# Routed attention: values taken in ten turns of a unit's 36 blocks, one turn across two rows' ends, and a weights' ring 15 slots deep

## The chip, the cores and the metric

One core of one Trainium2 chip. The metric is the device time of the program in microseconds. The kernel before has a median of 668.74 us over 3 runs (668.3 to 669.78).

## What is computed

`x` is 2 x 1024 tokens of 512 numbers. After a layer norm two attentions run on it and both are added to `x`:

- a local one, 16 query heads of 32 on 4 key heads, with biases, RMS norm, rotary position and a window of 64 keys back, then an output projection;
- a routed one. Each token has 16 heads of keys and values, of which a gate picks one (`argmax`), so all 16 query heads share one key and one value per token:

```
k_shared = einsum('bth,bthd->btd', indicator, k)
v_shared = einsum('bth,bthd->btd', gating_top1, v)
att = einsum('bhqd,bkd->bhqk', q, k_shared) / sqrt(hd)
att = softmax(where(causal, att, -inf))
y = einsum('bhqk,bkd->bhqd', att, v_shared)
```

The change is in the routed attention alone. All is float32, some matmuls in the float32r form.

## The kernel before, in words

The program has two stages. The first (layer norm, projections, local attention, output projection) ends where the routed attention begins, at 388.67 us of the profiled span. The order of the work on every engine comes from a planner (`make_plan`, then `Routed.run`), which keeps a model of the engines' times and writes out one list of steps; each engine's program walks this list and emits its own part of each step, with semaphore waits. TensorE executes in that order.

**Units, rows and blocks.** The routed attention is cut into 8 units u (4 groups of 4 heads by 2 batches). A unit has 8 rows i of 128 queries; row i has i + 1 key blocks j, the diagonal first, so 36 blocks k in all (`PRODUCTS`). The steps:

- `row_scores` (TensorE L1055, out `s_ps`, 4 banks): scores of a later unit, only for their row maxima, which VectorE takes (L1321, L1324). 48 for each unit but the first.
- `key_scores` (TensorE L1088, out `st_ps`, 3 banks): one float32r matmul of 512 columns for each block. ScalarE takes the exponential (L1545) into the weights' ring `p_t[k % RING]`, 12 slots; GpSimd zeroes what lies above the diagonal (L1684) and adds the weights of two neighbouring blocks into one of 6 `p_sum` buffers (L1697; in the last unit VectorE, L1350).
- `key_values` (TensorE L1104, out `od_ps`): for each block 4 matmuls of 32 output partitions, one for each head; the trace has 8 records for a block (a float32 matmul shows as two), and `key_sums` (L1118) the same for the row sums, one for each pair of blocks.
- `row_done` (ScalarE L1558): copy of a row's values and sums out of `od_ps`, 128 x 256.
- `finish` (TensorE L1127, out `s_ps`): two transposes, then VectorE divides (L1366, L1368); after every fourth row the residual is added and the unit's result is stored at its end.

**Turns.** TensorE takes `key_values` in turns of several blocks, between which it issues row scores, key scores and finishes. `value_group` cuts them inside a row: the row's rest when that is at most 5 blocks, else 4. That gives 1, 2, 3, 4, 5, 4 + 2, 4 + 3, 4 + 4: eleven turns a unit, 88 in all. A turn that begins a row waits for the copy of the row before (`ro_r`), since every row uses the same half, `od_ps[:, 0:2, :]`.

`Routed.run` takes the way that can start first of four: finish, maximum, key scores, values, with ties going in that order. Key scores are ready when a `st_ps` bank is free, the ring slot of 12 blocks before has been read and one of the 6 pair buffers is free; a turn of values when all its blocks are scored, its weights are ready and, for a row's start, the last copy is done.

Of the kernel before, what the change touches and what calls it, by code (L numbers as in the profile page):

```python
# [7 lines left out]
P = 128  # L8
D = 512
KC = D // P  # L10
H, HKV, DK = 16, 4, 32
# [68 lines left out]
HOP = 0.2  # L80

SLACK = 0.6
VALUES_AT_ONCE = 4

Q_LANDS = 6.0

# [379 lines left out]
    return p  # L466


def value_group(k):

    left = row_end(PRODUCTS[k][0]) - k + 1
    return left if left <= VALUES_AT_ONCE + 1 else VALUES_AT_ONCE


class Routed:
# [106 lines left out]
    def next_values(self):  # L582
        n = len(PRODUCTS)
        if self.valued == UNITS_ROUTED * n:
            return None
        u, k = divmod(self.valued, n)
        end = self.valued + value_group(k)
        if end > self.scored:
            return None
        whats = [self.done["weights", m] for m in range(self.valued, end)]  # L590
        i, j = PRODUCTS[k]
        if i == j:
            whats.append(self.values_free)
        if ends_row(k + value_group(k) - 1):
            whats += [self.done["pair", end - m] for m in (1, 2) if ("pair", end - m) in self.done]
        return max(whats)

    def take_values(self):
        n = len(PRODUCTS)
        self.now += TURN  # L600
        u, k = divmod(self.valued, n)
        _, hg, b = self.unit(u)
        i, j = PRODUCTS[k]
        for g in range(k, k + value_group(k)):
# [3 lines left out]
        if ends_row(g):  # L608
            for m in row_sums(i):
                self.do("key_sums", u, b, m)  # L610
                self.now += 0.22
                if m in PAIR_OF:
                    self.done["pair used", u * len(PAIR_OF) + PAIR_OF[m]] = self.now + HOP
                else:
                    self.done["sum", u * n + m] = self.now + HOP
            self.do("row_done", u, b, i)
# [3 lines left out]
        self.valued += g + 1 - k  # L620
        self.now += TURN

    def next_finish(self):
# [89 lines left out]
def mixed_attention_kernel(nc, counts, x, w_tok, w_qt, w_o, b_qkv, b_o, w_norm, scale, rope, ident, mask, rows, rank,  # L713
# [188 lines left out]
    def tensor_program(e):  # L902
        lane = Lane(e)
        for step, *key in plan.steps:
# [168 lines left out]
            elif step == "key_scores":  # L1073
                u, b, k = key
                i, j = PRODUCTS[k]
                if k == 0:
                    lane.wait_ge(*M["r_row"].of(u))
                    lane.wait_ge(*M["r_row_lo"].of(u))
                if u == 0:
                    lane.wait_ge(*queries(u, i))  # L1080
                if k >= ST_BANKS:
                    lane.wait_ge(*M["rp_exp"].of((u, k - ST_BANKS)))
                elif u:
                    lane.wait_ge(*M["rp_exp"].of((u - 1, len(PRODUCTS) - ST_BANKS + k)))
                else:

                    lane.wait_ge(*M["p_t_r"].of((*last_tile, k + 1)))
                e.matmul(st_ps[k % ST_BANKS][:, :, :], k_stack[0:HALVES + 2, b * S + j * P:b * S + (j + 1) * P],  # L1088
                         q_op[b][0:HALVES + 2, i, :, :], start=True, stop=True).then_inc(
                             *M["rst_mm"].did((u, k)))  # L1090

            elif step == "key_values":
                u, b, k = key
                i, j = PRODUCTS[k]
                if i == j:
                    lane.wait_ge(*M["rp_diag"].of((u, i)))
                    if i or u:
                        lane.wait_ge(*M["ro_r"].of((u, i - 1) if i else (u - 1, IT - 1)))
                    else:
                        lane.wait_ge(*M["at_lo"].of(last_tile))  # L1100
                else:
                    lane.wait_ge(*M["rp_exp"].of((u, k)))
                for h in range(HQ):
                    mm = e.matmul(od_ps[h * DK:(h + 1) * DK, 0, :], v_all[:, b * IT + j, 0:DK],  # L1104
                                  p_t[k % RING][:, h, :], start=i == j, stop=ends_row(k))
                mm.then_inc(*M["rpv"].did((u, k)))

            elif step == "key_sums":
                u, b, k = key
                i, j = PRODUCTS[k]  # L1110
                if k in PAIR_OF:
                    lane.wait_ge(*paired(u, k))
                    weights = p_sum[(u * len(PAIR_OF) + PAIR_OF[k]) % SUMS]
                else:
                    weights = p_t[k % RING]
                first = k == row_sums(i)[0]
                for h in range(HQ):
                    mm = e.matmul(od_ps[h * DK:(h + 1) * DK, 1, :], v_all[:, b * IT + j, DK:VW], weights[:, h, :],  # L1118
                                  start=first, stop=ends_row(k))
# [12 lines left out]
    def vector_program(e):  # L1132
# [3 lines left out]
        for step, *key in plan.steps:  # L1136
# [201 lines left out]
            elif step == "key_scores":  # L1338
                u, b, k = key
                i, j = PRODUCTS[k]  # L1340
                p = p_t[k % RING]
                if k in PAIR_OF and SUMMER[u] == "V":
                    lane.wait_ge(*M["rp_exp"].of((u, k)))
                    if PRODUCTS[k - 1][1] == i:
                        lane.wait_ge(*M["rp_diag"].of((u, i)))
                    n = u * len(PAIR_OF) + PAIR_OF[k]
                    if n >= SUMS:
                        w, was = divmod(n - SUMS, len(PAIR_OF))
                        lane.wait_ge(*M["rsum"].of((w, ENDS_PAIR[was])))
                    e.tensor_tensor(p_sum[n % SUMS][:, :, :], p_t[(k - 1) % RING][:, :, :], p[:, :, :],  # L1350
                                    ALU.add).then_inc(*M["rp_pair_v"].did((u, k)))

            elif step == "finish":
# [26 lines left out]
    def scalar_program(e):  # L1380
# [12 lines left out]
        for step, *key in plan.steps:  # L1393
# [135 lines left out]
            elif step == "key_scores":  # L1529
                u, b, k = key  # L1530
                lane.wait_ge(*M["rst_mm"].of((u, k)))
                if u == 0 and k < RING:

                    if k < 2 * RING_P_LOC:
                        lane.wait_ge(*M["p_t_r"].of((*last_tile, QUADS - 1)))
                    elif k < 2 * RING_P_LOC + QUADS:
                        lane.wait_ge(*M["pv_mm"].of(last_tile))
                    else:
                        lane.wait_ge(*M["gemm_read"].of((ROUNDS - 1, *LAST_UNIT)))
                if k >= RING or u:  # L1540
                    w, was = (u, k - RING) if k >= RING else (u - 1, len(PRODUCTS) - RING + k)
# [3 lines left out]
                e.activation(p_t[k % RING][:, :, :], st_ps[k % ST_BANKS][:, :, :], ACT.Exp, scale=ROUTED_SCALE).then_inc(  # L1545
                    *M["rp_exp"].did((u, k)))
# [21 lines left out]
    def gpsimd_program(e):  # L1568
# [6 lines left out]
        for step, *key in plan.steps:  # L1575
# [101 lines left out]
            elif step == "key_scores":  # L1677
                u, b, k = key
                i, j = PRODUCTS[k]
                p = p_t[k % RING]  # L1680
                if i == j:
                    lane.wait_ge(*M["rp_exp"].of((u, k)))
                    e.nop(nofuse=True)
# [3 lines left out]
                elif k in PAIR_OF and SUMMER[u] == "G":  # L1687
# [9 lines left out]
                    e.tensor_tensor(p_sum[n % SUMS][:, :, :], p_t[(k - 1) % RING][:, :, :], p[:, :, :],  # L1697
                                    ALU.add).then_inc(*M["rp_pair"].did((u, k)))

            elif step == "finish":  # L1700
# [223 lines left out]
```

## Time and profile before

| what | value |
|---|---|
| median of 3 runs | 668.74 us (668.3 to 669.78) |
| the profiled execution's own time | 671.4 us |
| its span | 669.5 us |
| mean granted TensorE clock | 0.993 |
| routed attention on TensorE | 388.67 to 664.02 us |
| TensorE, weight loads, VectorE, ScalarE, GpSimd busy | 95, 76, 68, 54, 66% of the span |

In the rows below PE is TensorE's matmuls and PEld its weight loads, DVE VectorE, ACT ScalarE, POOL GpSimd. Matmul ends are modelled, so the argument goes by starts. A group such as `x3` runs from its first start to its last modelled end.

### The profile page before, as it was taken

The numbers are of one execution on the slowest core, as the hardware profiler recorded it, in microseconds if no ns is written. First come the engines' busy times: TensorE is split into PE (matmuls) and PEld (weight loads), VectorE is DVE, ScalarE is ACT, GpSimd is POOL, SyncE is SP. The second block draws the span as 40 slices with busy tenths as digits, with TensorE's granted clock in tenths as the row PEclk, the third lists the DMA queues.
The fourth block names the chain that finished last, engine by engine and source line by source line (L and its number), as shares of the span: only waits on it lengthen the run. The fifth ranks groups of instructions, "written<-read, shape, count | busy, mean of one in ns | idle before, by whom it ended". The sixth has DMA issues, their size and how long they took to land.

```text
span 669.5 us, 19210 instructions
## 1 busy us (share of the span) xinstructions
PE 637.4 (95%) x7432; PEld 509.8 (76%) x7432; DVE 455.8 (68%) x1184; ACT 361.7 (54%) x906; POOL 442.4 (66%) x384
## 2 busy tenths in 40 slices
PE   4699999999999999999999899999999999999997
PEld 3587788887888888888778677777777777777675
DVE  3966457657665675656664388887878787878454
ACT  5357355625544445535257455656565565656684
POOL 3876856368654749382895467776878687868730
PEclk9999999999999999999999899999999999999999
DMA  9524222241223133212216631503214131302011
GB/s 315 197 60 112 60 77 79 76 122 41 78 70 91 50 94 104 78 39 75 64 33 166 163 96 58 137 26 93 71 51 113 51 111 36 104 29 89 4 34 33
DMA packets 64939, 56.59 MB, mean 85 GB/s; under 512 B 6480, under 2 KB 48848, under 8 KB 64848
## 3 DMA queue, kind: packets, MB, share of 16 engines
q1 hardware_dynamic: 62704, 54.45, 27.9%
q8 instruction: 58, 0.95, 0.6%
q10 hardware_dynamic: 2144, 0.93, 0.5%
q14 instruction: 33, 0.27, 0.1%
HBM read 37.20 MB, written 17.89 MB: 82 GB/s over the span
## 4 chain that ended last, share of the span: by engine, by line
PE 88%; DVE 5%; ACT 2%; DMA 2%; issue 2%; SPq 0%; ACTq 0%; DVEq 0%
PE gemm L946 20%; PE s_ps L1055 12%; PE od_ps L1104 11%; PE st_ps L1088 10%; PE gemm L1032 7%; PE gemm L942 6%; PE od_ps L1118 5%; PE win L1006 4%; PE win L991 3%; PE s_ps L1127 2%; PE av L1018 2%; DMA raw<-w_tok 2%; PE av L1045 1%; PE tp L957 1%; PE tp L913 1%
## 5 line engine op out<-in xcount | busy, mean ns | idle before, releaser
L946 PE MATMUL gemm<-w_tok,xt 128*128 128x512 f32 (+1 forms) x768 | 184.0, 380 | 5.4 <-DVE g_exp L1188 2.2
L946 PEld LDWEIGHTS gemm<-w_tok,xt 128*128 128x128 f32 x768 | 129.6, 191 | 28.5 <-DVE g_exp L1188 2.7
L1055 PE MATMUL s_ps<-k_stack,w_tok 96*128 96x512 f32 (+2 forms) x336 | 100.0, 381 | 0.3 <-DVE x_res L1286 0.3
L1088 PE MATMUL st_ps<-w_tok,k_stack 98*128 98x512 f32 x288 | 98.9, 413 | 0.2 <-ACT p_loc L1545 0.2
L1545 ACT ACTIVATE p_loc<-st_ps 128x512 f32<-128x512 f32 x144 | 77.6, 599 | 35.9 <-PE st_ps L1088 34.7
L1321 DVE TENSOR_REDUCE picked_fk<-s_ps 128x1 f32<-128x512 f32 x112 | 72.3, 684 | 9.0 <-PE s_ps L1055 8.9
L1497 ACT ACTIVATE p_loc<-win,l_max 128x96 f32<-128x96 f32 x256 | 60.9, 390 | 31.1 <-DVE l_max L1260 31.1
L1055 PEld LDWEIGHTS s_ps<-k_stack,w_tok 96*128 96x128 f32 x336 | 54.9, 188 | 24.6 <-issue 8.8
L1642 POOL TENSOR_TENSOR rope_b<-qkv,sin_t 128x128 f32<-128x128 f32 (+1 forms) x32 | 27.5, 880 | 65.5 <-DVE qkv L1238 65.5
L1666 POOL TENSOR_TENSOR p_loc<-p_loc,l_rec 128x1536 f32<-128x1536 f32 x16 | 44.1, 2758 | 36.4 <-DVE l_rec L1272 36.4
L1324 DVE CUSTOM_DVE_ANT_0 s_ps<-s_ps,x_ln,picked_fk 128x128 f32<-128x128 f32 (+3 forms) x112 | 56.8, 555 | 9.7 <-PE s_ps L1055 9.7
L1324 DVE CUSTOM_DVE_ANT_0 s_ps<-s_ps,x_ln 128x128 f32<-128x128 f32 (+3 forms) x112 | 51.8, 521 | 16.2 <-PE s_ps L1055 15.9
L1545 ACT ACTIVATE p_loc_t<-st_ps 128x512 f32<-128x512 f32 x96 | 52.3, 599 | 18.9 <-PE st_ps L1088 18.6
L942 PE MATMUL gemm<-xt,w_qt 128*128 128x256 f32 x384 | 55.0, 291 | 4.5 <-DVE g_exp L1188 2.8
L1088 PEld LDWEIGHTS st_ps<-w_tok,k_stack 98*128 98x128 f32 x288 | 50.6, 189 | 9.8 <-ACT p_loc L1545 2.1
L1618 POOL TENSOR_TENSOR rms_y<-rms_v,minus_half 128x20 f32<-128x20 f32 x16 | 56.5, 3534 | 1.3
L1032 PE MATMUL gemm<-w_o,attn_t 128*128 128x512 f32 x192 | 54.0, 414 | 2.4 <-DVE attn_t L1277 2.4
L942 PEld LDWEIGHTS gemm<-xt,w_qt 128*128 128x128 f32 x384 | 50.1, 195 | 7.6 <-DVE g_exp L1188 3.3
L1104 PE MATMUL od_ps<-p_loc,v_all 128*32 128x128 f32 x1152 | 44.3, 277 | 0.0
L1506 ACT ACTIVATE p_loc_t<-win 96x512 f32<-96x512 f32 x64 | 36.7, 638 | 13.8 <-PE win L1006 12.8
L1684 POOL TENSOR_SCALAR_AFFINE_SELECT p_loc<-p_loc 128x512 f32<-128x512 f32 x40 | 25.0, 634 | 25.3 <-ACT p_loc L1545 25.3
L1032 PEld LDWEIGHTS gemm<-w_o,attn_t 128*128 128x128 f32 x192 | 34.3, 193 | 9.4 <-issue 3.1
(172 smaller groups left out, 1295.4 us busy)
## 6 DMA issues: line engine op xcount, KB each, us to landing
w_tok<-q_parts SPq DMA_DIRECT2D x72, 128.0 KB, 2.6
q_parts<-qt SPq DMA_DIRECT2D x120, 64.0 KB
x_ln<-x SPq DMA_DIRECT2D x8, 512.0 KB, 4.6
x_res<-x SPq DMA_DIRECT2D x16, 256.0 KB, 2.8
partial<-x_res SPq DMA_DIRECT2D x16, 256.0 KB, 2.3
w_tok<-partial SPq DMA_DIRECT2D x8, 512.0 KB, 5.2
raw<-w_tok SPq DMA_DIRECT2D x3, 1024.0 KB, 12.5
v_win<-v_rows SPq DMA_DIRECT2D x64, 48.0 KB, 2.2
```

Of the source, the lines that this page charges most:

```text
L942: i = e.matmul(g[:, 0:PAIR], w_qt_p[r][:, k, a * P:(a + 1) * P], xs[l][:, k, :], start=first, stop=last)
L946: i = e.matmul(g[:, 0:cols], xs[l][:, k, a * P:(a + 1) * P], w_tok_p[r][:, k, c0:c0 + cols], start=first, stop=last)
L1032: i = e.matmul(gemm[bank][:, :], attn_t[l][:, kc, :], w_o_p[r][:, kc, :], start=kc == 0 and q == 0, stop=kc == KC - 1 and q == 2)
L1055: e.matmul(s_ps[bank][:, 0:cols], q_op[b][0:HALVES, i, h, :], k_stack[0:HALVES, b * S + c0:b * S + c0 + cols], start=True, stop=True).then ...
L1088: e.matmul(st_ps[k % ST_BANKS][:, :, :], k_stack[0:HALVES + 2, b * S + j * P:b * S + (j + 1) * P], q_op[b][0:HALVES + 2, i, :, :], start=T ...
L1104: mm = e.matmul(od_ps[h * DK:(h + 1) * DK, 0, :], v_all[:, b * IT + j, 0:DK], p_t[k % RING][:, h, :], start=i == j, stop=ends_row(k))
L1321: e.tensor_reduce(dst, s[:, 0:cols], AX.X, ALU.max).then_inc(*M["rs_max"].did((u, t)))
L1324: e.tensor_tensor_reduce(out=s[:, 0:cols], in0=s[:, 0:cols], in1=causal[:, S - width + c0:S - width + c0 + cols], scale=1.0, scalar=dst if ...
L1497: i = e.activation(p_loc[a][:, g, quad, :], win[:, g, quad * KEYS:(quad + 1) * KEYS], ACT.Exp, bias=l_max[:, a, n:n + 1])
L1545: e.activation(p_t[k % RING][:, :, :], st_ps[k % ST_BANKS][:, :, :], ACT.Exp, scale=ROUTED_SCALE).then_inc(*M["rp_exp"].did((u, k)))
L1618: e.tensor_tensor(rms_y[:, :], rms_v[:, :], minus_half[:, :].to_broadcast([P, NH]), ALU.pow).then_inc(*M["rms_r"].did((n, a)))
L1666: e.tensor_tensor(p_l, p_l, l_rec[:, a, :].unsqueeze(2).to_broadcast([P, H, KEYS]), ALU.mult).then_inc(*M["p_r"].did((m, a)))
```

## The change

It replaces the rule of the turns by a table of ten sizes, of which the first covers rows 0 and 1 (1 + 2 blocks); the other nine are the sizes of before. In a turn all values come first, then all sums, then the copies of the rows that end in it. Rows alternate between the two halves of the bank `od_ps`; a row's copy waits for the sums of the last row of its turn, and a turn's first diagonal waits for the copy of the row before the turn. The ring has 15 slots, three more in rooms that the first stage has left (two in `k_t`, one in `picked_fv`), and its slot goes on counting from unit to unit, since 36 is no multiple of 15.

```diff
-RING = 12
+RING = 15
+
+TURN_SIZES = (3, 3, 4, 5, 4, 2, 4, 3, 4, 4)
+TURN_OF = {}
+for _n in TURN_SIZES:
+    TURN_OF.update(dict.fromkeys(range(len(TURN_OF), len(TURN_OF) + _n), (len(TURN_OF), len(TURN_OF) + _n - 1)))
...
-def value_group(k):
-
-    left = row_end(PRODUCTS[k][0]) - k + 1
-    return left if left <= VALUES_AT_ONCE + 1 else VALUES_AT_ONCE
+def turn_end(k):
+
+    return TURN_OF[k][1] + 1
+
+
+def rows_ended(k):
+
+    return [i for i in range(IT) if k <= row_end(i) < turn_end(k)]
...
+def ring(u, k):
+    return (u * len(PRODUCTS) + k) % RING
...
-        whats = [self.done["weights", m] for m in range(self.valued, end)]
-        i, j = PRODUCTS[k]
-        if i == j:
-            whats.append(self.values_free)
-        if ends_row(k + value_group(k) - 1):
-            whats += [self.done["pair", end - m] for m in (1, 2) if ("pair", end - m) in self.done]
+        whats = [self.done["weights", m] for m in range(self.valued, end)] + [self.values_free]
+        whats += [self.done["pair", u * n + m] for i in rows_ended(k) for m in row_sums(i) if m in PAIR_OF]
...
+    keys_room = Room(k_t)
+    p_t += [keys_room.piece(HQ, P) for _ in range(2)] + [Room(picked["fv"]).piece(HQ, P)]
...
-                    if i or u:
-                        lane.wait_ge(*M["ro_r"].of((u, i - 1) if i else (u - 1, IT - 1)))
+                    first = PRODUCTS[TURN_OF[k][0]][0]
+                    if first or u:
+                        lane.wait_ge(*M["ro_r"].of((u, first - 1) if first else (u - 1, IT - 1)))
...
-                    mm = e.matmul(od_ps[h * DK:(h + 1) * DK, 0, :], v_all[:, b * IT + j, 0:DK],
-                                  p_t[k % RING][:, h, :], start=i == j, stop=ends_row(k))
+                    mm = e.matmul(od_ps[h * DK:(h + 1) * DK, 2 * (i % 2), :], v_all[:, b * IT + j, 0:DK],
+                                  p_t[ring(u, k)][:, h, :], start=i == j, stop=ends_row(k))
...
-                lane.wait_ge(*M["rsum"].of((u, row_end(i))))
+                lane.wait_ge(*M["rsum"].of((u, row_end(max(rows_ended(turn_of_row(i)[0]))))))
...
-                e.activation(o_sb[i % 2][:, :, :], od_ps[:, 0:2, :], ACT.Copy).then_inc(*M["ro_r"].did((u, i)))
+                e.activation(o_sb[i % 2][:, :, :], od_ps[:, 2 * (i % 2):2 * (i % 2) + 2, :], ACT.Copy).then_inc(*M["ro_r"].did((u, i)))
```

## Rows read from the trace of the kernel before

**Rows 1.** The page: span and busy time.

```profile
span 669.5 us, 19210 instructions
...
PE 637.4 (95%) x7432; PEld 509.8 (76%) x7432; DVE 455.8 (68%) x1184; ACT 361.7 (54%) x906; POOL 442.4 (66%) x384
```

**Rows 2.** The page: the chain that ended last, shares by engine.

```profile
PE 88%; DVE 5%; ACT 2%; DMA 2%; issue 2%; SPq 0%; ACTq 0%; DVEq 0%
```

**Rows 3.** Windows: stretch, PE, PEld, DVE, ACT, POOL busy (x), clock, DMA share, GB/s.

```profile
388.67:664.02 275.35, 274.38 (x4326) 204.44 (x4325) 212.31 (x702) 173.05 (x352) 195.18 (x185) 1.00 0.24 65
425.44:609.66 184.22, 183.66 (x2766) 137.21 (x2765) 149.87 (x510) 113.33 (x231) 142.47 (x135) 1.00 0.28 75
626.87:662.22 35.35, 35.04 (x675) 25.70 (x674) 15.25 (x37) 27.65 (x58) 15.00 (x17) 1.00 0.07 18
```

**Rows 4.** Waits in the routed stage: who waited for whom, total us, times, longest.

```profile
PEld od_ps L1104 <- issue: 22.0, 78, 0.4
```

**Rows 5.** Timeline of PE: one turn of values in the last unit.

```profile
652.85 0.97 PE L1088 MATMUL st_ps<-w_tok,k_stack 98*128 98x512 f32 x3
653.74 0.64 PE L1104 MATMUL od_ps<-p_loc_t,v_all 128*32 128x128 f32 x16
...
654.42 0.40 PE L1118 MATMUL od_ps<-bias_o,v_all 128*32 128x128 f32 x8
654.64 0.40 PE L1118 MATMUL od_ps<-cos_t,v_all 128*32 128x128 f32 x8
654.97 0.96 PE L1088 MATMUL st_ps<-w_tok,k_stack 98*128 98x512 f32 x3
```

**Rows 6.** Timeline of PE: a gap with row scores and seven key scores.

```profile
600.38 1.19 PE L1055 MATMUL s_ps<-k_stack,w_tok 96*128 96x512 f32 x4
601.41 0.62 PE L1088 MATMUL st_ps<-w_tok,k_stack 98*128 98x512 f32 x2
601.93 0.47 PE L1055 MATMUL s_ps<-k_stack,w_tok 96*128 96x512 f32 x1
602.24 0.39 PE L1088 MATMUL st_ps<-w_tok,k_stack 98*128 98x512 f32 x1
...
604.41 0.30 PE L1055 MATMUL s_ps<-k_stack,w_tok 96*128 96x256 f32 x1
604.64 0.62 PE L1104 MATMUL od_ps<-p_loc_t,v_all 128*32 128x128 f32 x13
```

**Rows 7.** Timeline of PE: a gap without row scores and with five key scores.

```profile
635.21 0.96 PE L1088 MATMUL st_ps<-w_tok,k_stack 98*128 98x512 f32 x3
636.40 0.98 PE L1088 MATMUL st_ps<-w_tok,k_stack 98*128 98x512 f32 x2 [0.22 <-ACT p_loc L1545]
637.31 0.43 PE L1104 MATMUL od_ps<-p_loc_t,v_all 128*32 128x128 f32 x8
```

**Rows 8.** Windows of L1088 alone: stretch, PE busy (x key scores), PEld busy (x).

```profile
626.87:662.22 35.35, 14.94 (x45) 7.35 (x45) 1.00 0.07 18
611.27:613.82 2.55, 0.80 (x2) 0.38 (x2) 1.00 0.47 144
425.44:609.66 184.22, 62.96 (x186) 32.90 (x185) 1.00 0.28 75
...
600.30:604.64 4.34, 2.43 (x7) 1.32 (x7) 1.00 0.31 93
```

**Rows 9.** Timeline, all engines: end of row 1's turn, its copy, row 2's turn.

```profile
642.48 0.40 PE L1118 MATMUL od_ps<-bias,v_all 128*32 128x128 f32 x8
642.81 0.96 PE L1088 MATMUL st_ps<-w_tok,k_stack 98*128 98x512 f32 x3
642.94 0.39 ACT L1558 ACTIVATE rope_b<-od_ps 128x256 f32<-128x256 f32 x1
643.92 0.54 PE L1104 MATMUL od_ps<-p_loc,v_all 128*32 128x128 f32 x12
```

**Rows 10.** Windows of L1055 alone, the same columns: row scores in the long gap.

```profile
600.30:604.64 4.34, 3.29 (x9) 1.60 (x9) 1.00 0.31 93
```

More of the change, by code:

```diff
@@ L82 @@
 SLACK = 0.6
-VALUES_AT_ONCE = 4
 Q_LANDS = 6.0
@@ L586, in next_values @@
         u, k = divmod(self.valued, n)
-        end = self.valued + value_group(k)
+        end = u * n + turn_end(k)
         if end > self.scored:
             return None
-        whats = [self.done["weights", m] for m in range(self.valued, end)]
-        i, j = PRODUCTS[k]
-        if i == j:
-            whats.append(self.values_free)
-        if ends_row(k + value_group(k) - 1):
-            whats += [self.done["pair", end - m] for m in (1, 2) if ("pair", end - m) in self.done]
+        whats = [self.done["weights", m] for m in range(self.valued, end)] + [self.values_free]
+        whats += [self.done["pair", u * n + m] for i in rows_ended(k) for m in row_sums(i) if m in PAIR_OF]
         return max(whats)
@@ L602, in take_values @@
         _, hg, b = self.unit(u)
-        i, j = PRODUCTS[k]
-        for g in range(k, k + value_group(k)):
+        rows = rows_ended(k)
+        for g in range(k, turn_end(k)):
             self.do("key_values", u, b, g)
@@ L607, in take_values @@
             self.done["values", u * n + g] = self.now + HOP
-        if ends_row(g):
+        for i in rows:
             for m in row_sums(i):
@@ L615, in take_values @@
                     self.done["sum", u * n + m] = self.now + HOP
+        for i in rows:
             self.do("row_done", u, b, i)
@@ L619, in take_values @@
             self.values_free = self.copied[u * IT + i] = self.busy(self.now + 0.1, ("A", 0.38)) + HOP
-        self.valued += g + 1 - k
+        self.valued += turn_end(k) - k
         self.now += TURN
@@ L1114, in tensor_program @@
                 else:
-                    weights = p_t[k % RING]
+                    weights = p_t[ring(u, k)]
                 first = k == row_sums(i)[0]
                 for h in range(HQ):
-                    mm = e.matmul(od_ps[h * DK:(h + 1) * DK, 1, :], v_all[:, b * IT + j, DK:VW], weights[:, h, :],
+                    mm = e.matmul(od_ps[h * DK:(h + 1) * DK, 2 * (i % 2) + 1, :], v_all[:, b * IT + j, DK:VW], weights[:, h, :],
                                   start=first, stop=ends_row(k))
@@ L1340, in vector_program @@
                 i, j = PRODUCTS[k]
-                p = p_t[k % RING]
+                p = p_t[ring(u, k)]
                 if k in PAIR_OF and SUMMER[u] == "V":
@@ L1349, in vector_program @@
                         lane.wait_ge(*M["rsum"].of((w, ENDS_PAIR[was])))
-                    e.tensor_tensor(p_sum[n % SUMS][:, :, :], p_t[(k - 1) % RING][:, :, :], p[:, :, :],
+                    e.tensor_tensor(p_sum[n % SUMS][:, :, :], p_t[ring(u, k - 1)][:, :, :], p[:, :, :],
                                     ALU.add).then_inc(*M["rp_pair_v"].did((u, k)))
@@ L1537, in scalar_program @@
                         lane.wait_ge(*M["pv_mm"].of(last_tile))
-                    else:
-                        lane.wait_ge(*M["gemm_read"].of((ROUNDS - 1, *LAST_UNIT)))
-                if k >= RING or u:
-                    w, was = (u, k - RING) if k >= RING else (u - 1, len(PRODUCTS) - RING + k)
+                    elif k < 2 * RING_P_LOC + QUADS + 2:
+                        lane.wait_ge(*M["gemm_read"].of((ROUNDS - 1, *LAST_UNIT)))
+                    elif k < 2 * RING_P_LOC + QUADS + 4:
+                        lane.wait_ge(*M["s_mm"].of(last_tile))
+                    else:
+                        lane.wait_ge(*M["picked_fv"].of(last_tile))
+                if u or k >= RING:
+                    w, was = divmod(u * len(PRODUCTS) + k - RING, len(PRODUCTS))
                     lane.wait_ge(*M["rpv"].of((w, was)))
@@ L1544, in scalar_program @@
                     lane.wait_ge(*(paired(w, done) if done in PAIR_OF else M["rsum"].of((w, done))))
-                e.activation(p_t[k % RING][:, :, :], st_ps[k % ST_BANKS][:, :, :], ACT.Exp, scale=ROUTED_SCALE).then_inc(
+                e.activation(p_t[ring(u, k)][:, :, :], st_ps[k % ST_BANKS][:, :, :], ACT.Exp, scale=ROUTED_SCALE).then_inc(
                     *M["rp_exp"].did((u, k)))
@@ L1679, in gpsimd_program @@
                 i, j = PRODUCTS[k]
-                p = p_t[k % RING]
+                p = p_t[ring(u, k)]
                 if i == j:
@@ L1696, in gpsimd_program @@
                         lane.wait_ge(*M["res_bias"].of(last_tile))
-                    e.tensor_tensor(p_sum[n % SUMS][:, :, :], p_t[(k - 1) % RING][:, :, :], p[:, :, :],
+                    e.tensor_tensor(p_sum[n % SUMS][:, :, :], p_t[ring(u, k - 1)][:, :, :], p[:, :, :],
                                     ALU.add).then_inc(*M["rp_pair"].did((u, k)))
```

2 lines of the change are left out of this document (added).

## The prediction

> **What bounds the kernel now.** I read the page's busy line and chain first: TensorE is busy 95% of the span and holds 88% of the chain that ended last [rows 1, 2]. Busy time alone proves little, so I cut the span into stretches. From 388.67 to 664.02 us, the routed stage, matmuls cover 274.38 of 275.35 us at granted clock 1.00, the upper of the two levels (2.4 GHz), while VectorE has 212.31 and ScalarE 173.05 [rows 3]. Nothing else is near full, in units 1 to 5 or in the stretch without row scores. So the stage is as long as TensorE's issue order takes, and the question is how much of it goes into switching and waiting instead of into columns. The waits give a first hint: 78 of the 88 turns begin with weight loads idle on "issue", 22.0 us together, 0.28 us each [rows 4]. It is overlapped in part, so I don't take it as the price; I take starts in the timeline.
>
> **Price of a turn.** In the chosen turn the third key score starts at about 652.85 + 0.97 - 0.39 = 653.43 (0.39 is the modelled length of a single one), the values at 653.74: 0.31 us later [rows 5, 6]. Two key scores in a row start 0.62 - 0.39 = 0.23 apart [rows 6]. Entry costs 0.08. At the end, groups of eight sums start 0.22 apart, so the next would be at 654.86; the key score comes at 654.97, 0.11 late. And three key scores behind a turn take 0.96 instead of 0.39 + 2 x 0.23 = 0.85: 0.11 more [rows 5]. Together **0.30 us a turn**. The change has 80 turns for 88: gross **-2.4 us**. The blocks' own matmuls don't change in number or shape.
>
> **What the merged turn moves.** It needs both rows' three blocks at once, two diagonal cuts and one pair sum; blocks run several ahead of values nearly everywhere, so I price this at nothing; without that lead it would cost the exponential and the cut of block 2. On ScalarE the copy of row 0 now stands directly before that of row 1, with the exponentials behind both. Row 2's turn waits for both, where it waited for one. A copy is 0.39 us. Before, it starts at 642.94, 0.46 after the last sums' first start, and row 2's turn starts at 643.92 [rows 9]. A second copy would end at 643.72, 0.20 before the turn: just covered by three key scores and a finish. I take 0; if uncovered, 8 x 0.39 = 3.1 us, the other end. The two finishes come together and take two of the four `s_ps` banks, a delay for row scores, not more of them. No DMA issue is added. Those tied to key scores (query loads on SyncE's queue) can only come earlier with a longer lead, those tied to a row's copy in unit 0 about one gap later; the first is not needed for a unit, the second for a residual added four rows later. GpSimd's cuts and sums keep number and order among themselves.
>
> The copies are also the place where a rule speaks. The Trainium skill, page "PSUM — Partial Sum Buffer", section "PSUM bank collisions raise a hardware error", says that TensorE writing and ScalarE reading one bank in the same partitions collide even at different columns. The alternation of halves inside one bank would by this buy no overlap of values and copy, and with no cover behind it the sum would be 3.1 us worse; the trace has no such overlap to judge it by.
>
> **What fewer gaps cost.** This is the counter-term. Between turns TensorE fills with row scores and key scores, and there are three `st_ps` banks. The stretch without row scores has 45 key scores in its 15 gaps, exactly three a gap [rows 8]. A unit needs 36: eleven gaps hold 33 at three each, ten hold 30, so six instead of three must be a fourth or later in a gap (or done in advance). Their price, from below and above:
> - without row scores: from the third key score at 635.21 + 0.96 - 0.39 = 635.78 to the turn at 637.31 is 1.53 us; two more at 0.23 and the way into the turn, 0.31, would be 0.77 [rows 7]. So 0.76 is lost, 0.38 for each beyond three;
> - with row scores between: the gap from 600.38 has 9 row scores and 7 key scores, 16 instructions [rows 8, 10]. 15 pitches of 0.23, 0.10 behind the turn and 0.21 from the narrow last one make 3.76; it took 4.26 [rows 6]. 0.50 over 4 is 0.12 each. The lower end is 0, since units 1 to 5 hold 186 key scores in 55 gaps, 3.4 a gap, with TensorE covering 183.66 of 184.22 us [rows 3, 8]. I take 0.05, near the lower end, because most gaps there hold a fourth key score and only the longest ones show much.
> Three more a unit, in some seven units with row scores: 21 x 0.05 = **+1.05 us** (0 to 2.5).
>
> **What the deeper ring gives.** At the start of unit 6 the gap has only two key scores [rows 8] though three banks exist: twelve slots are full. Three more slots let the lead grow there. The six pair buffers bound it next: with rows 6 and 7 holding seven pairs, about 14 blocks ahead. The lead is spent at the end, where the last 45 must fit 14 gaps (42). Before, the lead ran short once, at the 0.76 us gap [rows 7]. I take half of that back, **-0.4 us** (0 to -0.76). In unit 0 the first lap is also freer, by blocks 12 to 14; nothing before unit 0's sums depends on it, so 0.
>
> **Sum:** -2.4 + 1.05 - 0.4 = -1.75 us. The profiled execution took 671.4 us, of which 669.5 is span; it would be 669.65. The median shown is 668.74, 2.7 us below that execution, an offset I keep: **667.0 us**. Before 388.67 and behind the last turn nothing changes.
>
> **Rivals.**
> 1. *All of the saving and the long gaps too*: the lead stays high enough that later key scores cost nothing. For it: the capped gap at unit 6 shows room for more; against it: ten gaps of three are 30, not 36. -2.4 - 0.76, about 665.6.
> 2. *Turns saved, waits gained*: each unit pays 3 x 0.12 = 0.36 for 0.30 saved. Against it: VectorE and ScalarE have a fifth or more idle [rows 3]. For it: four and three banks are a shallow queue, and rows 6 show it empty. 21 x 0.12 = 2.5 against 2.4 and perhaps 0.2 from the ring: 668.6. This is also where it ends if the planner, whose order I haven't got, trades the turn for longer gaps.
> 3. *The end stretch starves (slower)*: place, the key scores from the last row score on. If the lead there isn't larger than before, 3 more key scores in this stretch and 3 in unit 6 behind it pay 0.38: 2.3 us, besides 2.5 of rival 2. +4.8 - 2.4 = 671.1. It decides where the gaps there must hold more than three; with a lead of eleven or more it doesn't come.
> 4. *Two copies in a row hold up row 2's turn*: uncovered, +3.1 on -1.75, 670.1. Against it: the 0.20 us of cover just worked out, more in units with row scores. By the bank rule above the wait can't be avoided, only covered.
> The change not doing what it says has one form, that a turn across a row's end costs a switch inside; values and sums alternate in today's turns with starts as even as within either (the 0.22 of rows 5), so I leave it out.
>
> **How the numbers follow.** Forecast 0.50, rival 1 0.13, rival 2 0.22, rival 3 0.11, rival 4 0.04. The forecast's own range is 665.9 to 667.8, from the bounds 0 and 0.12 of the later key scores narrowed by the ring's. Two tenths of a per cent, 1.3 us, is about what a measurement of this kernel can tell from no change; that is 667.4 or 670.1. Faster: 0.42 of the forecast's half and rival 1, 0.55. Slower: rival 3 and half of rival 4, 0.13. Within: 0.32. The range leaves out the far part of rival 3 and of rival 4 and a little below rival 1: 665.2 to 669.3.
>
> **What would show it.** Right: 80 groups of values instead of 88, each with 0.30 around it; unit starts about 0.15 to 0.3 us closer together; capped gaps of two gone; last turn near 660.5 instead of 662.22. A chain still on TensorE. Wrong: key scores with idle time ended by ScalarE in many gaps (rivals 2 and 3), counts of five and more in gaps without row scores (3), the weight load before row 2's first values idle on the copy (4), or unit lengths unchanged though turns are gone. If the total moves by more than 3.2 us, something other than turns moved.

## The result, and the profile after

After: **675.07 us** (673.79 to 678.17, 4 runs); before, 668.52 (668.29 to 669.78, 4 runs). The ratio is 1.0085, 95% interval 1.0048 to 1.0121: slower, by some 6 us, where 667.0 was forecast and 669.3 was the upper end of the range. The profiled execution took 674.89 us. Its page, span, busy time and chain:

```profile
span 673.6 us, 19202 instructions
...
PE 641.5 (95%) x7432; PEld 510.6 (76%) x7432; DVE 456.8 (68%) x1184; ACT 361.9 (54%) x906; POOL 445.7 (66%) x384
...
PE 86%; DVE 5%; ACT 3%; issue 2%; DMA 2%; POOL 1%; SPq 0%; ACTq 0%; DVEq 0%; POOLq 0%
```

Against [rows 1, 2] this tells little: TensorE is still busy 95% of the span, 4.1 us longer, and holds 86% of the chain for 88. So the stage has to be cut. Windows of the kernel after, by the first values of a unit: unit 0; units 1 to 5; units 6 and 7 up to the start of the last sums, in two lines; the whole stage; and a stretch behind unit 0's end. The columns are those of [rows 3]:

```profile
386.04:428.38 42.34, 40.95 (x565) 30.74 (x564) 35.36 (x123) 24.53 (x50) 28.89 (x28) 0.96 0.34 91
428.38:610.79 182.41, 181.58 (x2746) 134.02 (x2746) 142.77 (x486) 110.73 (x226) 136.33 (x129) 1.00 0.27 70
610.79:645.57 34.78, 34.67 (x574) 25.39 (x573) 21.91 (x66) 21.53 (x46) 26.21 (x26) 1.00 0.08 23
645.57:668.12 22.55, 22.28 (x445) 16.19 (x444) 14.35 (x30) 16.39 (x33) 3.08 (x5) 1.00 0.09 26
386.04:668.12 282.08, 279.48 (x4326) 206.33 (x4325) 214.39 (x702) 173.18 (x352) 194.51 (x185) 0.99 0.24 64
...
421.37:427.00 5.63, 5.63 (x19) 4.74 (x20) 4.58 (x15) 4.26 (x8) 5.35 (x6) 0.70 0.59 159
```

The kernel before: unit 0, and units 6 and 7 in two lines, of which only the sum is compared (units 1 to 5 are the second line of [rows 3]):

```profile
388.67:425.44 36.77, 36.67 (x554) 27.29 (x554) 31.54 (x112) 21.41 (x44) 23.97 (x23) 1.00 0.22 64
609.66:640.32 30.66, 30.35 (x519) 22.01 (x518) 17.64 (x51) 20.18 (x43) 23.97 (x23) 1.00 0.13 38
640.32:664.02 23.70, 23.70 (x491) 17.95 (x490) 13.27 (x31) 18.14 (x38) 4.78 (x6) 1.00 0.09 25
```

Unit 0 took 42.34 us for 36.77, units 1 to 5 182.41 for 184.22, units 6 and 7 57.33 for 54.36. The stage is +6.73: +5.6, -1.8, +3.0. (The profiled span is only 4.1 longer because the stage started 2.63 us earlier; see the last section.)

These three numbers can't be read as they stand, since the stretches don't hold the same work. A unit's first values now stand behind more scores, of its own and of the unit after it. The counts of TensorE's records in the rows say by how much: 565 for 554 in unit 0, 2746 for 2766 in units 1 to 5, 574 + 445 for 519 + 491 in units 6 and 7, so +11, -20 and +9. By starts, these are 6 key scores and 5 row scores more in unit 0, 5 and 15 fewer in units 1 to 5, 1 fewer and 10 more behind them. At 0.23 us each (an estimate, the pitch of two key scores) that moves +2.5, -4.6 and +2.1 us. At equal work unit 0 lost some 3.0 us, the five middle units 2.8, and the last two 0.9: all three stretches lost, the middle ones too.

TensorE's covered time grew too, from 274.38 to 279.48, with the same 4326 matmul records: only 2.6 us of the stage are idle, and the instructions stand further apart.

Turns themselves, waits of the weight loads, and two new waits of TensorE; then the waits of the row scores' weight loads on VectorE, after and before:

```profile
PEld od_ps L1122 <- issue: 17.7, 60, 0.5
...
PE st_ps L1105 <- DMA w_tok<-w_tok: 1.1, 1, 1.1
PE od_ps L1122 <- ACT rope_sq L1580: 0.8, 5, 0.2
...
PEld s_ps L1072 <- DVE picked_fk L1342: 11.7, 47, 0.3
...
PEld s_ps L1055 <- DVE picked_fk L1324: 5.5, 24, 0.3
```

60 turns for 78 of [rows 4] begin with that idle time, 0.30 us each. The second line is where the matter shows: a key score waits for the DMA that brings the row of maxima of its unit. That wait is in no group of the prediction. The third is a turn that waits for the copy of the row before it, once in each of the units 1 to 5.

### The profile page after: what moved, and what is told of

Its sections match the earlier page's. It is cut to its first block, busy times and chain, and to the rows that moved or that the text cites. A ratio compares the mean times of both kernels' runs of the same rounds, so it can differ in the third digit from the quotient of the medians.

```text
span 673.6 us, 19202 instructions
## 1 busy us (share of the span) xinstructions
PE 641.5 (95%) x7432; PEld 510.6 (76%) x7432; DVE 456.8 (68%) x1184; ACT 361.9 (54%) x906; POOL 445.7 (66%) x384
## 4 chain that ended last, share of the span: by engine, by line
PE 86%; DVE 5%; ACT 3%; issue 2%; DMA 2%; POOL 1%; SPq 0%; ACTq 0%; DVEq 0%; POOLq 0%
PE gemm L963 20%; PE s_ps L1072 12%; PE od_ps L1122 11%; PE st_ps L1105 10%; PE gemm L1049 6%; PE gemm L959 6%; PE od_ps L1136 5%; PE win L1023 4%; PE win L1008 3%; PE av L1035 2%; PE s_ps L1145 2%; DMA raw<-w_tok 2%; PE av L1062 1%; PE tp L974 1%; PE tp L930 1%
## 5 line engine op out<-in xcount | busy, mean ns | idle before, releaser
L1105 PE MATMUL st_ps<-w_tok,k_stack 98*128 98x512 f32 x288 | 108.1, 422 | 1.1 <-DMA w_tok<-w_tok 1.1
L1072 PE MATMUL s_ps<-k_stack,w_tok 96*128 96x512 f32 (+2 forms) x336 | 106.4, 387 | 0.3 <-DVE x_res L1304 0.3
L1072 PEld LDWEIGHTS s_ps<-k_stack,w_tok 96*128 96x128 f32 x336 | 56.1, 190 | 29.1 <-DVE picked_fk L1342 11.7
L1567 ACT ACTIVATE p_loc<-st_ps 128x512 f32<-128x512 f32 x117 | 63.5, 604 | 21.3 <-PE st_ps L1105 21.1
L1105 PEld LDWEIGHTS st_ps<-w_tok,k_stack 98*128 98x128 f32 x288 | 51.5, 191 | 13.1 <-issue 4.9
L1049 PE MATMUL gemm<-w_o,attn_t 128*128 128x512 f32 x192 | 52.6, 406 | 2.4 <-DVE attn_t L1295 2.4
L1567 ACT ACTIVATE p_loc_t<-st_ps 128x512 f32<-128x512 f32 x76 | 41.7, 602 | 12.7 <-PE st_ps L1105 12.6
L1524 ACT ACTIVATE p_loc_t<-win 96x512 f32<-96x512 f32 x64 | 36.8, 640 | 12.1 <-PE win L1023 11.2
L1023 PE MATMUL win<-idt,p_loc 128*96 128x128 f32 x256 | 37.7, 272 | 0.0
L1670 POOL TENSOR_TENSOR qkv<-qkv,cos_t 128x128 f32<-128x128 f32 (+1 forms) x32 | 29.3, 937 | 11.1 <-ACT rope_sq L1472 10.1
```

The source lines that it names most:

```text
L1023: i = e.transpose(win[0:KEYS, quad, g * P:(g + 1) * P], p_loc[a][:, g, quad, :], idt[:, :])
L1049: i = e.matmul(gemm[bank][:, :], attn_t[l][:, kc, :], w_o_p[r][:, kc, :], start=kc == 0 and q == 0, stop=kc == KC - 1 and q == 2)
L1072: e.matmul(s_ps[bank][:, 0:cols], q_op[b][0:HALVES, i, h, :], k_stack[0:HALVES, b * S + c0:b * S + c0 + cols], start=True, stop=True).then ...
L1567: e.activation(p_t[ring(u, k)][:, :, :], st_ps[k % ST_BANKS][:, :, :], ACT.Exp, scale=ROUTED_SCALE).then_inc(*M["rp_exp"].did((u, k)))
```

## What the trace after shows at a unit's end

Key scores (L1105, 1088 before) alone: from the start of unit 5's last-but-one turn to that of its last turn (602.39), and from there to unit 6's first turn (610.79):

```profile
600.65:602.39 1.74, 0.00 (x0) 0.00 (x0) 1.00 0.46 131
602.39:610.79 8.40, 4.49 (x12) 2.25 (x12) 1.00 0.24 71
```

In 600.65 to 602.39 there is no key score at all; the next stretch, which holds the last turn of unit 5 and the long gap behind it, has 12, with some 13 row scores. Before, the gap in front of unit 5's last turn held seven [rows 8] and the one behind it five. All 36 key scores of a unit are out before the planner has the row of maxima of the next one, and between the turns that are left stand a few row scores and finishes, but no key score; in unit 6, whose end has no row scores left, nothing stands between the last two turns. Counted from the starts, the lead of key scores over values falls from 8 to 4 to 0 over these turns, in each of the units 0 to 6; before, it fell to 0 at unit 0's end and never under 3 in the units 1 to 6. In the units 1 to 5 TensorE itself never stands for the row: it is the planner's order that answers to it.

The long gap that follows is not where the time goes: its 27 matmuls (12 key scores, 13 row scores, a finish) take 6.7 us, 0.25 each. Two other places are seen. One key score is left before the last-but-one turn, which begins row 7 and has to wait for the copy of row 6:

```profile
599.98 0.50 PE L1105 MATMUL st_ps<-w_tok,k_stack 98*128 98x512 f32 x1
600.65 0.43 PE L1122 MATMUL od_ps<-k_t,v_all 128*32 128x128 f32 x8 [0.16 <-ACT rope_sq L1580]
```

The way into the turn is 0.67 us there for the 0.31 that the prediction found, so 0.36 more, and it is 0.67 in all five units: 1.8 us. And row scores that follow one another wait for VectorE, 11.7 us of idle weight loads for 5.5 (in e5 of the experiments it is 4.2); how much of that is covered isn't known.

At unit 0's end the row is also late. The chain of the kernel after, in order of time (start, length, what), and TensorE's timeline there:

```profile
417.81 0.14 DVE w_tok L1353
417.96 0.02 issue
417.97 3.26 DMA w_tok<-w_tok
421.23 0.14 issue
421.37 0.47 PE st_ps L1105
```

```profile
419.87 0.41 PE L1145 MATMUL s_ps<-idt,rope_b 128*128 128x128 f32 x2 [0.30 <-DVE picked_fk L1342]
421.37 0.47 PE L1105 MATMUL st_ps<-w_tok,k_stack 98*128 98x512 f32 x1 [1.09 <-DMA w_tok<-w_tok]
...
423.76 0.63 PE L1105 MATMUL st_ps<-w_tok,k_stack 98*128 98x512 f32 x1
424.18 0.63 PE L1072 MATMUL s_ps<-k_stack,w_tok 96*128 96x512 f32 x1
424.61 0.63 PE L1105 MATMUL st_ps<-w_tok,k_stack 98*128 98x512 f32 x1
425.04 0.63 PE L1072 MATMUL s_ps<-k_stack,w_tok 96*128 96x512 f32 x1
425.46 0.60 PE L1105 MATMUL st_ps<-w_tok,k_stack 98*128 98x512 f32 x1
...
426.37 0.40 PE L1072 MATMUL s_ps<-k_stack,w_tok 96*128 96x512 f32 x1
426.60 0.40 PE L1105 MATMUL st_ps<-w_tok,k_stack 98*128 98x512 f32 x1
```

VectorE's last step ends at 417.95, the row lands at 421.23, and TensorE stands for 1.4 us in all (0.30 and 1.09). The planner counts 2.6 us from VectorE's end to a usable row; it took 3.4. Then the granted clock is 0.70 over 5.63 us, between the upper level (2.4 GHz) and the lower (1.2), and between 423.76 and 425.46 starts are 0.43 us apart instead of 0.23. The clock granted 0.30 of 5.63 us less, 1.7 us; e1 below, with the same order in unit 0, takes 1.69 us less in unit 0, 0.44 of it a shorter wait. So the fall cost some 1.3 to 1.7 us. The Trainium skill, page "TensorE: Matmul & The Clock Gate", section "Wait — 56ns, not 53.3ns?", gives 426.7 ns from start to start for 512 columns at the lower level; the trace agrees.

At the other end, units 6 and 7, TensorE's and ScalarE's timelines of the gap before the last unit's merged turn, and behind it:

```profile
639.86 0.97 PE L1105 MATMUL st_ps<-w_tok,k_stack 98*128 98x512 f32 x3
640.67 0.38 PE L1145 MATMUL s_ps<-idt,rope_b 128*128 128x128 f32 x2
641.05 1.97 PE L1105 MATMUL st_ps<-w_tok,k_stack 98*128 98x512 f32 x4
642.95 0.65 PE L1122 MATMUL od_ps<-k_t,v_all 128*32 128x128 f32 x16
...
643.85 0.40 PE L1136 MATMUL od_ps<-bias,v_all 128*32 128x128 f32 x8
```

```profile
641.85 2.08 ACT L1567 ACTIVATE p_loc<-st_ps 128x512 f32<-128x512 f32 x4
644.32 0.38 ACT L1580 ACTIVATE rope_sq<-od_ps 128x256 f32<-128x256 f32 x1 [0.38 <-PE od_ps L1136]
644.60 0.38 ACT L1580 ACTIVATE rope_b<-od_ps 128x256 f32<-128x256 f32 x1
```

Seven key scores in one gap without row scores; before, the 45 in 15 gaps of [rows 8] stood three to a gap but for one gap of five [rows 7] and the last of one. The last four take 1.97 us, 0.49 a pitch, the pace of four exponentials (2.08): with three `st_ps` banks TensorE can't run ahead. Row 0's and row 1's copies start 0.47 and 0.75 after the start of the last sums (643.85), and row 2's turn comes at 645.57, 0.59 after the second copy's end.

## The experiments

The theory, after this reading: **the loss is the wait for the row of maxima**. With fewer gaps the key scores of a unit are used up sooner, but the 48 row scores that the next row of maxima needs are spread over one gap fewer, hence later. The wait is meant in two forms: TensorE standing, and the order that the planner makes of it. Rivals: the deeper ring; the turn across two rows; the longer gaps by themselves. Since stage one differs by up to 5.7 us between profiled executions, I give for each run, beside the ratio, the stage's length from the first values' start to the last sums' start, in the profiled execution. Before: 275.3; after: 282.1. It is one execution each; after's units 2 to 5, of the same make, take 36.49 to 36.53 us, so the length repeats well within an execution, but a fall of the clock can be in it.

**Undo one of the two parts.** e1 keeps the ten turns; e2 keeps the ring, and gives rows 0 and 1 turns of their own:

```diff
-RING = 15
+RING = 12
```
```diff
-TURN_SIZES = (3, 3, 4, 5, 4, 2, 4, 3, 4, 4)
+TURN_SIZES = (1, 2, 3, 4, 5, 4, 2, 4, 3, 4, 4)
```

> The changed kernel with the ring back at 12 slots and its ten turns a unit. Theory A (the ten turns of these sizes make key scores run out at every unit's end, since the next unit's row of maxima isn't there yet): the ring has no part in it, ratio to the kernel before 1.007 to 1.012, about 674 to 676 us, and a gap with some 12 key scores before each unit's first turn. Theory B (the three new slots, in rooms of the first stage or by a longer lead, cause it): within 0.3% of the kernel before.

> The changed kernel with the eleven turns of before (1, 2, 3, 4, 5, 4, 2, 4, 3, 4, 4) and the ring of 15 slots, rows alternating in od_ps. Theory A: no loss, 0.997 to 1.001 of the kernel before, since row 0's turn and its gap are back. Theory B (ring or alternating halves at fault): 1.005 or more.

e1: 675.07 us, 1.009 (1.0057 to 1.0122), stage 280.6: nearly all of the loss is there without the ring. e2: 667.46 us, 0.9983 (0.9959 to 1.0006), stage 274.4: no loss without the merged turn, and perhaps 0.9 us from the ring. The ring as the cause falls; what is left is the turns.

**Is it the merged turn, or where the gaps lie?** e3 and e4 keep ten turns and the merged one, and cut the last row 3, 5, with 12 and 15 slots.

```diff
-TURN_SIZES = (3, 3, 4, 5, 4, 2, 4, 3, 4, 4)
+TURN_SIZES = (3, 3, 4, 5, 4, 2, 4, 3, 3, 5)
```

> Ten turns as in the change but for the last two, 3 and 5 blocks in place of 4 and 4, and a ring of 12 slots. Same number of turns as the changed kernel, but the order on TensorE has the next unit's row of maxima in time from unit 1 on. Theory A: most of the loss goes, but unit 0's end still waits once: 0.995 to 1.002 of the kernel before. Theory C (fewer gaps are the price themselves: a fourth key score in a gap waits for ScalarE whatever the order): 1.006 or more, as in the changed kernel.

> The same last turns of 3 and 5 blocks with 15 slots. In TensorE's order key scores then run three blocks further ahead, reach the unit's end earlier and again find no row of maxima. Theory A: slow like the changed kernel, 1.007 to 1.014, and by over 0.7% slower than the same turns with 12 slots. Theory C: no difference between the two rings beyond 0.3%.

e3: 669.5 us, 0.9993 (0.9963 to 1.0023), stage 275.1. e4: 675.6 us, 1.0109 (1.0058 to 1.016), stage 281.7. The same turns, 6.6 us of stage apart by three ring slots (1.5 of it in unit 0, where e4's clock fell); with the 4, 4 cut the ring had mattered by 1.5 only. So neither the merged turn nor the number of turns costs 6 us, and the ring isn't harmless either: a deeper one lets key scores be issued sooner and be used up sooner. Their units 1 to 5 take 36.5 us each in after, e1 and e4, 35.4 to 35.7 in e3. The first key score behind the row, and the windows of the next stretch, e1, e3 and e4 in this order:

```profile
421.20 0.47 PE L1105 MATMUL st_ps<-w_tok,k_stack 98*128 98x512 f32 x1 [0.65 <-DMA w_tok<-w_tok]
...
421.20:427.00 5.80, 5.79 (x28) 4.18 (x32) 5.36 (x20) 5.29 (x11) 5.14 (x6) 1.00 0.52 136
```
```profile
422.71 0.47 PE L1105 MATMUL st_ps<-w_tok,k_stack 98*128 98x512 f32 x1 [1.19 <-DMA w_tok<-w_tok]
...
422.71:428.50 5.79, 5.79 (x29) 4.19 (x33) 5.13 (x21) 5.28 (x11) 4.34 (x5) 1.00 0.28 78
```
```profile
423.73 0.47 PE L1105 MATMUL st_ps<-w_tok,k_stack 98*128 98x512 f32 x1 [1.41 <-DMA w_tok<-w_tok]
...
423.73:428.70 4.97, 4.97 (x17) 4.28 (x18) 3.65 (x13) 3.61 (x7) 3.60 (x4) 0.66 0.17 49
```

All three wait for the row, so all have a long unit 0 (40.6, 40.5, 42.0 us for 36.8, of which some 2.4 are the 10 or 11 scores more that stand in it). The clock fell in e4 and in after, and stayed at 1.00 in e1 and e3. e3's wait of 1.19 is longer than after's 1.09 (which follows another of 0.30), so the length of this one wait doesn't decide it. The 1.5 us of difference between after and e1 lies in unit 0 alone (42.34 and 40.65): it is the clock's and 0.44 us of a longer wait, and the other seven units differ by 0.2 in all.

**Take the wait away.** In e5 the row of maxima is free from the start for every unit: the planner has it ready, key scores wait for unit 0's row alone, which is written to both batches' places, and the later rows go to a spare tensor in HBM. What this changes in the computation: units 1 to 7 use unit 0's maxima. The work of the compute engines stays. e6 is the same with eleven turns and 12 slots.

```diff
-        self.row_ready = {0: p.now}
+        self.row_ready = {u: p.now for u in range(UNITS_ROUTED)}
...
-        self.row_ready[u] = end + 2.6
...
-                if k == 0:
+                if k == 0 and u == 0:
...
+                if u:
+                    e.dma_start(spare[u, 1], r_max_t[:, 1, :].bitcast(F32)).then_inc(*M["r_row_lo"].did(u, inc=16))
```

> The changed kernel (ten turns, 15 slots), but key scores of units 1 to 7 don't wait for their row of maxima, neither in the planner nor in the kernel: unit 0's row is written for both batches and the later rows are sent to a spare place in HBM, so the maxima are computed and moved as before but not used. Theory A: the loss is the wait for that row, so this is 0.993 to 0.999 of the kernel before. Theory C (fewer gaps): still 1.004 or more.

> The same freeing of the row of maxima with the eleven turns and 12 slots of before: the companion of the run before. By the price of a turn from the prediction (0.30 us, 8 turns) it should be 2.4 us slower than the ten turns without the wait, less if gaps of more than three key scores cost; so ten over eleven 0.995 to 0.999. If it is the faster one of the two, the turns' saving doesn't exist even without the wait. Against the kernel before: 0.996 to 1.000.

The stage of e5, e6 and, below, of e9 and e10:

```profile
387.00:660.23 273.23, 272.92 (x4326) 204.98 (x4325) 213.38 (x702) 173.02 (x352) 195.78 (x185) 1.00 0.24 66
```
```profile
388.00:662.03 274.03, 273.28 (x4326) 204.59 (x4325) 212.23 (x702) 172.65 (x352) 195.37 (x185) 1.00 0.24 65
```

e5: 668.75 us, 0.9994 (0.9971 to 1.0016). e6: 668.25, 0.9992 (0.997 to 1.0013). The 6 us are gone from the ten turns. But the times don't tell the two apart (lowest 666.94 and 666.82): e6 was expected to be 0.1 to 0.5% slower than e5, and by the medians it isn't; e5's 0.9994 is also just above what was expected. That ten turns are worth anything here stands on the stages alone, which split the whole: the row's wait and the order it forces cost 275.35 - 274.03 = 1.32 with eleven turns, 282.08 - 273.23 = 8.85 with ten; that is +7.53. The turns and the ring themselves (e5 has 15 slots, e6 12) give 274.03 - 273.23 = 0.80. 7.53 - 0.80 = 6.73, the stage's loss.

**What is a turn worth, then?** Again with free rows (units 1 to 7 on unit 0's maxima) and 12 slots: nine turns in e9, thirteen in e10.

```diff
+TURN_SIZES = (3, 3, 4, 5, 6, 4, 3, 4, 4)
```
```diff
+TURN_SIZES = (1, 2, 3, 2, 2, 3, 2, 3, 3, 4, 3, 4, 4)
```

> The row of maxima not waited for, as before, with nine turns a unit (3, 3, 4, 5, 6, 4, 3, 4, 4) and 12 slots. If a turn's 0.30 us were saved in full, the routed stage would be 2 x 8 x 0.30 = 4.8 us shorter than with eleven turns, about 269 us. If what a dropped turn saves is spent again in gaps that hold more scores than banks, it is 273 to 277 us long: no shorter than with eleven (274.0) or ten (273.2).

> The same with thirteen turns a unit (1, 2, 3, 2, 2, 3, 2, 3, 3, 4, 3, 4, 4), 104 in all and 12 slots. Gaps are then short and the scores fit the banks, so the added turns should cost their full price: 16 more than with eleven at 0.30 us is +4.8, a stage of about 277 to 279 us. If turns had no price of their own, it would stay at 274.

```profile
385.53:658.22 272.69, 272.68 (x4325) 205.84 (x4325) 212.59 (x702) 172.08 (x352) 194.65 (x185) 1.00 0.24 66
```
```profile
391.26:668.27 277.01, 276.93 (x4325) 202.92 (x4325) 212.27 (x702) 174.09 (x352) 195.58 (x185) 1.00 0.24 64
```

e9: 667.62 us, 0.9968 (0.9945 to 0.9992). e10: 672.1, 1.0034 (1.0007 to 1.0061). Per turn: 2.98 over 16 = 0.19 us from thirteen to eleven, 0.80 over 8 = 0.10 from eleven to ten, 0.54 over 8 = 0.07 from ten to nine. From thirteen to nine the times say the same as the stages: 0.66% or 4.4 us, and 4.3. Thirteen were expected to cost the full 0.30 each, and didn't. Of the price of 0.30, two thirds or more are not saved once there are eleven or fewer; that they go into the longer gaps is likely, not shown. These are single profiled stages, so the 0.10 and 0.07 are not told apart.

**Does a version beat both?** With a table for each unit, more turns can stand where the row is late or the end is short of key scores, and fewer in the middle. e7 (15 slots) and e8 (12), the tables alone shown:

```diff
-TURN_SIZES = (3, 3, 4, 5, 4, 2, 4, 3, 4, 4)
+TURN_SIZES = [(1, 5, 4, 5, 4, 2, 5, 2, 4, 4), (1, 2, 3, 4, 5, 3, 3, 3, 4, 3, 5),
+              (3, 3, 4, 5, 6, 3, 4, 8), (3, 3, 4, 5, 6, 5, 2, 8), (3, 3, 4, 5, 6, 4, 3, 8),
+              (3, 3, 4, 5, 6, 4, 3, 8), (3, 3, 4, 5, 3, 3, 4, 3, 5, 3),
+              (1, 2, 3, 2, 2, 5, 4, 2, 3, 4, 5, 3)]
```
```diff
+RING = 12
+TURN_SIZES = [(1, 2, 7, 5, 3, 3, 5, 2, 5, 3), (1, 5, 4, 5, 3, 3, 3, 4, 4, 4),
+              (3, 3, 4, 5, 6, 4, 3, 5, 3), (3, 3, 4, 5, 6, 4, 3, 5, 3), (3, 3, 4, 5, 6, 4, 3, 5, 3),
+              (3, 3, 4, 5, 6, 4, 3, 5, 3), (3, 3, 4, 2, 3, 3, 3, 5, 2, 4, 4),
+              (1, 2, 3, 2, 2, 5, 3, 3, 3, 4, 5, 3)]
```

> A table of turns for each unit: 75 turns in all, mostly nine in units 2 to 5, twelve in the last, chosen so that on TensorE's order the next unit's row of maxima comes before the key scores run out, and with many short turns where no row scores are left; 15 slots. Theory A (turns save if key scores never run out): faster than the kernel before, 0.990 to 0.997. Theory C (fewer turns cost by themselves): 1.003 or more, since it has fewer turns than the changed kernel.

> Another table for each unit, about 80 turns, made in the same way for a ring of 12 slots. Theory A: 0.992 to 0.998 of the kernel before, up to 0.2% behind the 15 slots. Theory C: 1.002 or more.

e7: 668.03 us, 0.9985 (0.9963 to 1.0008), stage 273.5, with eight turns in each of units 2 to 5 (its expectation counts nine). e8: 668.55, 0.9987 (0.9963 to 1.0011), stage 273.3. Some 2 us of stage, and a total that can't be told from no change; both miss what was expected of them (up to 0.997 and 0.998). e11 and e12 also tell the planner that the row takes 3.5 us instead of 2.6: e11 with a new table, e12 with e2's eleven turns; both with 15 slots.

```diff
-        self.row_ready[u] = end + 2.6
+        self.row_ready[u] = end + 3.5
...
+TURN_SIZES = [(1, 2, 3, 4, 5, 3, 3, 4, 3, 3, 5), (1, 2, 3, 4, 5, 3, 3, 4, 3, 3, 5),
+              (3, 3, 4, 5, 3, 3, 3, 4, 8), (1, 5, 4, 5, 4, 2, 7, 4, 4), (3, 3, 4, 5, 6, 4, 3, 8),
+              (3, 3, 4, 5, 6, 5, 2, 8), (3, 3, 4, 5, 2, 4, 5, 2, 4, 4),
+              (1, 2, 3, 2, 2, 5, 4, 2, 5, 2, 5, 3)]
```

> A third table for each unit (78 turns, 15 slots), with the planner's estimate for the landing of the row of maxima raised from 2.6 to 3.5 us, since the trace of the changed kernel shows key scores starting 3.4 us behind the end of its last VectorE step. Theory A: the routed stage is 272 to 273.5 us, with unit 0 under 37.5; 0.993 to 0.998 of the kernel before. If unit 0 or 1 is still over 38 us, the row's landing wasn't what delays them.

> Eleven turns in every unit and 15 slots, as in the second experiment, with the estimate at 3.5 us. If the ring's deeper lead alone is what gained 0.9 us of stage there, the stage is again 274 to 275 us and the ratio 0.997 to 1.000; if that was chance of the order, it is 275 to 276.

e11: **666.91 us** (665.44 to 669.82, 12 runs) against 669.45 before, 0.9958 (0.9937 to 0.998). It beats both kernels; its stage:

```profile
386.04:658.57 272.53, 272.09 (x4326) 204.04 (x4325) 211.83 (x702) 172.89 (x352) 195.72 (x185) 1.00 0.24 66
```

e12: 667.85, 0.997 (0.9948 to 0.9992), but its stage of 274.7 is only 0.6 shorter than before's and 0.3 longer than e2's. So the 3.5 alone shows no gain in the stage, and that of e11 goes with its table; the table with 2.6 wasn't run. e11's units 4 and 5 have ten key scores in one gap and take 35.4 to 35.6 us, so a gap that holds many isn't what costs. e12's median is better than its stage explains; its lowest time, 667.29 for 667.76 before, is 0.5 less and agrees with it.

## Why the prediction was wrong

- **The step that failed** is in "What the merged turn moves" and "What fewer gaps cost": I kept the order of before, took one gap out of each unit and priced the key scores left over by how well they are covered. I took for granted that there are always key scores to issue. They are gated by the next unit's row of maxima, which hangs on 48 row scores that pass through four `s_ps` banks. With these turns the row is later than the key scores last; with one block moved between the last two turns and 12 slots (e3) it isn't, behind unit 0. That gate isn't in the sum, nor in a rival. By the stages it costs 7.53 us more with ten turns (and 15 slots) than with eleven (and 12).
- **What it does to the sum**: some 3.0 us at unit 0's end, where TensorE stands 1.4 us and the clock takes another 1.3 to 1.7; 2.8 in the middle units, where the copy of row 6 is no longer covered (some 1.8 of it) and row scores crowd; 0.9 in the last two. The copy was taken at 0 because three key scores and a finish cover it; it is uncovered where those run out, at row 6's end and not behind the merged turn.
- **The signal was in the code and the trace of before**: the wait for the row at a unit's first key score; the end of unit 0, where the lead fell to 0 in the kernel before too, so that "the lead ran short once, at the 0.76 us gap" was a wrong reading; and seven key scores in one gap at 600.38 [rows 6, 8], of which all but the first are the next unit's. I read the seven as a full queue; they look like the catching-up behind the row. The "exactly three a gap" was a mean: [rows 7] is one of those 15 gaps and has five. I wrote that I hadn't got the planner's order and took that for a matter of a few tenths; it was the largest unknown and deserved a bound of its own.
- **Price of a turn, 0.30 us**: nothing shows that the price at the switch is another (the weight loads sit idle 0.30 us a turn, for 0.28), but it is wrong as a saving. Less than a turn's price comes back: 0.80 us measured for what I summed as -2.4 + 1.05 - 0.4 = -1.75. Rival 2 would explain that, with a size between its own and mine.
- **The ring**, -0.4: eleven turns and 15 slots gave -0.9 of stage and 0.9983 (0.9959 to 1.0006), so size and sign can't be called wrong there. As a term that only adds, it was: with the 3, 5 cut it turned 275.1 into 281.7.
- **Rival 3**: what it describes came, seven and five key scores in gaps without row scores, and units 6 and 7 are +3.0 us (I had 2.3 for it). But 2.1 of the 3.0 are nine more scores in that stretch, and the seven in one gap come from the wait for unit 7's row, not from a lead that was always that small: with the rows free (e5) these two units take 56.0 us, with e3 56.8, for 57.3. Its condition, "with a lead of eleven or more it doesn't come", was no help: the lead was 11 at the turn behind the last row score (632.40), and 0 at that unit's end.
- **Rival 4** and the copies: as worked out. The first starts 0.47 after the last sums (0.46 given), the second 0.28 behind it rather than 0.39, and three key scores cover both; row 2's turn never waits for it (0.59 us of cover in the last unit). What the prediction cites there on PSUM banks was not tried: in every run a copy waits for its turn's sums, so none shows what an overlap would do.
- "If the total moves by more than 3.2 us, something other than turns moved": it did, and that pointed the right way.

What stays open: unit 0's +5.6 is nearly added up, by 1.4 idle, 1.3 to 1.7 of the clock and 2.5 of scores moved into it; of the 2.8 us of the middle units 1 is not placed. And why the clock fell behind a wait in two runs and not in three others.

## What to carry to other kernels

When an edit takes a slot out of a repeated order, list for each kind of filler what releases it, and follow the one with the longest release chain to the next iteration: the fillers run out there first, and the price is a wait, not the fraction of a pitch that the removed slot was worth. When stretches of two orders are compared, count the instructions in them first. A deeper buffer ahead of such a gate can make it worse, since it uses up the fillers sooner. And the price of a switch was here an upper end of what its removal gave; measure one count more and one fewer with the gate taken away.

## What was not expected of the hardware

- **The clock fell behind a short wait.** 1.4 us with nothing for TensorE to do (two finish matmuls inside, in after) was followed by a stretch near the lower level: by the granted 0.70 of 5.63 and 0.66 of 4.97 us some 3.4 us of it, with 19 and 17 matmul records where e1 and e3 have 28 and 29 in 5.8. It costs about as much again as the wait, and came in two of the five runs that waited for the row, after (1.09 us) and e4 (1.41), and not in e1 (0.65), e3 (1.19) and e8 (0.64).
- **Stage one, the same code in all kernels, ended between 385.5 and 391.3 us** of the profiled span. One stretch of it, before (first) and after:

```profile
370.00:380.00 10.00, 8.47 (x70) 6.75 (x68) 3.19 (x5) 2.99 (x7) 3.98 (x2) 0.83 0.80 206
```
```profile
370.00:380.00 10.00, 8.22 (x96) 6.04 (x89) 2.35 (x6) 5.02 (x10) 5.23 (x4) 1.00 0.81 209
```

The clock is 0.83 in before, e6, e7 and e10 and 1.00 in the other ten, and a heavy transfer (0.59 to 0.84 of the DMA engines) runs with it in either case. Here too a short wait of TensorE stands just ahead, 1.53 us in all fourteen; the nine matmuls behind it, before (first) and after:

```profile
373.51 3.73 PE L1032 MATMUL gemm<-w_o,attn_t 128*128 128x512 f32 x9 [1.53 <-DVE attn_t L1277]
```
```profile
372.46 2.33 PE L1049 MATMUL gemm<-w_o,attn_t 128*128 128x512 f32 x9 [1.53 <-DVE attn_t L1295]
```

They take 1.4 us longer in before. So the same wait in the same code brings the clock down in four executions of fourteen. Stage one puts 3 us and more between two executions of the same code, half of what is studied here; the length of the changed stage is the cleaner measure.
- **A 16 KB row from SBUF to SBUF** took 3.3 us from issue to landing on SyncE's queue at unit 0's end (2.1 on ScalarE's), against 2.4 and 2.1 in the kernel before at the same place, where it had the time.
